# Layer 0 of a graph network on one core: the sums of a tile in two products over 33 rows of 17 terms, instead of three products over two arrays

## The reference, cut to what matters

```python
h = jnp.maximum(_layernorm(x, axis=-1), 0.0)
x = x + _L0_gnn_ref(h, edge_weight, edge_attr_3, edge_index, w1, b1, w2, b2)
h = jnp.maximum(_layernorm(x, axis=-1), 0.0)
x = x + _L1_gnn_ref(h, edge_index, W1, b1, W2, b2, W3, b3)   # three convolutions
# inside _L0_gnn_ref
R = jax.nn.relu(abs_distances[:, None] @ w1 + b1) @ w2 + b2
...
acc = acc + _NORM[i] * jnp.einsum('euv,ef,evi,ofi->euo', Rb[..., k], Yf, Fb, C)
...
out = out.at[dst].add(msg)
```

## Time and profile before

| what | value |
|---|---|
| runs | 8066.38 us median, 8041.97 to 8079.02 |
| span of the profiled execution | 8083.0 us, first to last instruction |
| PE busy, PE weight loads | 5256.2 us (65%), 3511.6 us (43%) |
| DVE, ACT, POOL busy | 3618.0 us, 2730.5 us, 3513.2 us |
| line 1926, the sums of layer 0, PE matmuls | 1134.5 us busy, 9408 records |
| line 1370, the reduction of the slots on DVE | 196 instructions |

### The profile page before, as it was taken

The page is one execution under the profiler, slowest core; times in us unless marked ns, Lnnn a source line. Parts: engine busy times, 40 slices in busy tenths (PEclk is TensorE's granted clock), DMA queues, the critical chain, the costliest instruction groups (busy, mean ns, idle before and its releaser), DMA issues.

```text
span 8083.0 us, 169450 instructions
## 1 busy us (share of the span) xinstructions
PE 5256.2 (65%) x62463; PEld 3511.6 (43%) x62464; DVE 3618.0 (45%) x8469; ACT 2730.5 (34%) x6550; POOL 3513.2 (43%) x3660
## 2 busy tenths in 40 slices
PE   4777677776767775554544557777777778455555
PEld 2444344443434443333333345555555556333333
DVE  6666566665656656444444442222222223333334
ACT  3333333333333333444444432222222223222222
POOL 5545445444444542444444434333333332444442
PEclk8877788787877776555555567887777788565566
DMA  2111111111111113222222221111111112222223
GB/s 66 26 26 27 24 26 27 26 26 24 27 24 26 26 25 37 59 55 55 55 55 55 55 80 55 57 56 53 56 55 53 55 55 83 68 79 81 78 82 87
DMA packets 494908, 400.37 MB, mean 50 GB/s; under 512 B 269575, under 2 KB 454828, under 8 KB 493537
## 3 DMA queue, kind: packets, MB, share of 16 engines
q10 hardware_dynamic: 146996, 207.67, 7.6%
q0 software_dynamic: 115712, 109.02, 7.1%
q1 hardware_dynamic: 231536, 74.48, 4.2%
HBM read 375.52 MB, written 15.29 MB: 48 GB/s over the span
## 4 chain that ended last, share of the span: by engine, by line
PE 38%; another core or an unknown queue 22%; DVE 18%; issue 17%; ACT 2%; DVEq 1%; DMA 1%; ACTq 0%; SPq 0%
PE radial L2051 14%; PE sums L1926 5%; DVE scratch L1344 4%; DVE scratch L1336 4%; PE sums L2137 4%; PE psX L2066 3%; PE psT L2066 3%; PE radial L1911 2%; PE psX L2069 2%; DVE scratch L1354 2%; PE psT L2069 1%; DVE shared L1310 1%; PE radial L2033 1%; PE radial L1908 1%
## 5 line engine op out<-in xcount | busy, mean ns | idle before, releaser
L768 POOL DMA_INDIRECT rows<-table,idx x3616 | 3486.8, 964 | 4415.6 <-PE sums L2137 2099.7
L2051 PE MATMUL radial<-arena,shared 128*32 128x96 bf16 (+1 forms) x31200 | 1469.7, 283 | 1072.6 <-issue 907.8
L2051 PEld LDWEIGHTS radial<-arena,shared 128*32 128x32 bf16 (+1 forms) x31200 | 848.1, 120 | 1551.6 <-issue 1311.4
L1926 PE MATMUL sums<-scratch,onehot 128*64 128x264 f32 (+1 forms) x9408 | 1134.5, 393 | 378.2 <-DVE scratch L1361 207.2
L1926 PEld LDWEIGHTS sums<-scratch,onehot 128*64 128x64 f32 x9408 | 818.2, 161 | 924.6 <-issue 480.7
L834 ACT ACTIVATE dist<-iota,rel 128x64 f32<-128x64 f32 (+1 forms) x2368 | 619.5, 342 | 1190.4 <-PE sums L1926 790.0
L1597 DVE TENSOR_SCALAR shared<-scratch,line 128x640 bf16<-128x640 bf16 (+1 forms) x906 | 408.3, 451 | 1367.9 <-remote 1102.7
L991 ACT CAST scratch<-radial 128x480 bf16<-128x480 f32 x860 | 470.8, 556 | 1593.4 <-remote 985.1
L1911 PE MATMUL radial<-shared 64*128 64x384 f32 x3136 | 880.9, 583 | 81.4 <-issue 77.8
L1336 DVE TENSOR_TENSOR scratch<-radial,shared 128x512 f32<-128x512 f32 x784 | 536.4, 684 | 740.4 <-remote 704.1
L1344 DVE TENSOR_TENSOR scratch<-radial,shared 128x768 f32<-128x768 f32 x784 | 741.6, 946 | 0.0
(11 more groups left out here) (236 smaller groups left out, 5445.4 us busy)
## 6 DMA issues: line engine op xcount, KB each, us to landing
scratch<-places_d ACTq DMA_DIRECT2D x242, 800.0 KB
rows<-table,idx POOLq DMA_INDIRECT x3616
shared<-in_edge_weight SPq DMA_DIRECT2D x390, 128.0 KB
idx<-in_src SPq DMA_DIRECT2D x451, 4.0 KB
table<-arena SPq DMA_DIRECT2D x24, 256.0 KB, 2.7
table<-arena SPq DMA_DIRECT2D x2, 1176.0 KB, 10.6
accT<-in_edge_attr SPq DMA_DIRECT2D x2, 1152.0 KB
table<-arena SPq DMA_DIRECT2D x24, 96.0 KB, 2.0
```

Source lines behind the costliest of these rows:

```text
L768: (pool.indirect_dma_start(rows_3[:, r, j, :] if n in (1, 3) else rows[:, r, j, 0:WIDTH[n]], None, tables[n], bass.IndirectOffsetOnAxis(ap ...
L1926: last = nc.tensor.matmul(there, onehot[:, u % 2, 4 * h + t, 0:SW], taken_from, start=(h + q + part == 0), stop=(h == 1 and q == 1 and par ...
L2051: last = nc.tensor.matmul(d, from_src[n][:, h, i, t, :], table_of(n, s), start=True, stop=True, tile_position=(0, 32 * i))
```

## The change

The two arrays become one: 8 scalar rows and 33 output rows of 17 terms each, `terms[..., row, term]`. Rows 0 to 7 are the scalars, rows 8 to 40 the outputs; term 16 of an output is what lay in the tail (a zero, the 1 of the count, or the direction term). A tile takes 17 x 41 = 697 values instead of 689. PE sums a tile in two products: first terms 8 to 16 into all 9 slots of each output (297 columns), then terms 0 to 7 into the first 8 of the 9 slots (264 columns). The rest follows from that: line 1370 reduces 33 x 9 slots, the DVE views have rows of 16 at a distance of 17, and line 1361 writes its 24 values of a tile 17 apart instead of next to each other. The far windows (a branch that is taken when a group's destinations don't fit in two windows of 64 nodes) use the same two products. No wait, no semaphore and no order between engines is changed.

```diff
-SEG0 = 16 * MUL
-TAIL0 = SEG0 + 16 * OUTS
-MSGW = TAIL0 + OUTS
-SUMW = 8 * OUTS
+TERMS = 17
+FIRST = MUL
+VECTOR = FIRST + MUL + 1
+MSGW = TERMS * (FIRST + OUTS)
+SLOTS_0 = 9
+SUMW = SLOTS_0 * OUTS
...
+        terms = scratch[:, 0:2 * 4 * MSGW].rearrange("p (h t m s) -> p h t m s", h=2, t=4, s=TERMS)
...
                     prod = v.tensor_tensor(
-                        msg[:, h, t:t + 2, 0:2 * SEG0].rearrange("p t (m s) -> p t m s", s=16),
+                        terms[:, h, t:t + 2, 0:2 * MUL, 0:16],
...
                     last = v.tensor_tensor(
-                        msg[:, h, t:t + 2, SEG0 + 16 * (MUL + 1):TAIL0].rearrange("p t (n s) -> p t n s", s=16),
+                        terms[:, h, t:t + 2, VECTOR:FIRST + OUTS, 0:16],
...
-                v.tensor_reduce(coef[:, h, :, :], msg[:, h, :, 0:SEG0].rearrange("p t (u s) -> p t u s", s=16),
+                v.tensor_reduce(coef[:, h, :, :], terms[:, h, :, 0:MUL, 0:16],
...
-                term = msg[:, h, :, TAIL0 + MUL + 1:MSGW].rearrange("p t (i u) -> p t i u", i=3)
+                term = terms[:, h, :, VECTOR:FIRST + OUTS, TERMS - 1].rearrange("p t (i u) -> p t i u", i=3)
...
-                v.tensor_reduce(nodes[:, :], sums[:, u % 2, 0:SUMW].rearrange("p (o s) -> p o s", s=8),
+                v.tensor_reduce(nodes[:, :], sums[:, u % 2, 0:SUMW].rearrange("p (o s) -> p o s", s=SLOTS_0),
...
-                slots = there.rearrange("p (o s) -> p o s", s=8)
-                terms = msg[:, h, t, SEG0:TAIL0].rearrange("p (o s) -> p o s", s=16)
-                if part == 2:
-                    return slots[:, :, 0], msg[:, h, t, TAIL0:MSGW]
-                return slots, terms[:, :, 8 * part:8 * part + 8]
+                slots = there.rearrange("p (o s) -> p o s", s=SLOTS_0)
+                summands = terms[:, h, t, FIRST:FIRST + OUTS, :]
+                return slots[:, :, 0:8 + part], summands[:, :, 8 * part:8 + 9 * part]
...
-                    for part in range(3):
+                    for part in (1, 0):
                         for w in range(2):
                             t = 2 * q + w
                             there, taken_from = window_part(sums[w * SW:(w + 1) * SW, u % 2, 0:SUMW], h, t, part)
                             last = nc.tensor.matmul(there, onehot[:, u % 2, 4 * h + t, 0:SW], taken_from,
-                                                    start=(h + q + part == 0), stop=(h == 1 and q == 1 and part == 2),
+                                                    start=(h + q == 0 and part == 1), stop=(h == 1 and q == 1 and part == 0),
                                                     tile_position=(0, w * SW))
```

More of the change, by code:

```diff
@@ L1242, in _ @@
             dve.wait_ge(table_out[0], 48)
-            link(v.memset(msg[:, :, :, SEG0 + 16 * MUL:SEG0 + 16 * MUL + 16], 0.0))
-            link(v.memset(msg[:, :, :, TAIL0:TAIL0 + MUL], 0.0))
-            link(v.memset(msg[:, :, :, TAIL0 + MUL:TAIL0 + MUL + 1], 1.0))
+            link(v.memset(terms[:, :, :, FIRST + MUL, 0:TERMS - 1], 0.0))
+            link(v.memset(terms[:, :, :, FIRST:FIRST + MUL, TERMS - 1], 0.0))
+            link(v.memset(terms[:, :, :, FIRST + MUL, TERMS - 1:TERMS], 1.0))
             dve.wait_ge(repeated, 2)
@@ L1288, in far_windows @@
                         if n == 0:
-                            v.tensor_reduce(nodesX[:, :], psX[:, 0:SUMW].rearrange("p (o s) -> p o s", s=8),
+                            v.tensor_reduce(nodesX[:, :], psX[:, 0:SUMW].rearrange("p (o s) -> p o s", s=SLOTS_0),
                                             X, ALU.add).then_inc(far_nodes, 1)
@@ L1881, in far_windows @@
                             if n == 0:
-                                for part in range(3):
+                                for part in (1, 0):
                                     there, taken_from = window_part(psX[:, 0:SUMW], j // 4, j % 4, part)
                                     last = nc.tensor.matmul(there, onehotX[:, j, :], taken_from,
-                                                            start=(j + part == 0), stop=(j == TPG - 1 and part == 2))
+                                                            start=(j == 0 and part == 1), stop=(j == TPG - 1 and part == 0))
                             elif far_rows[j] is not None:
```

## The result

The changed kernel takes 8219.61 us, the median of five runs (8170.37 to 8251.88), and the kernel before 8064.02 us in five runs beside them: a ratio of 1.019, 95% interval 1.0156 to 1.0224. It is slower, by 1.6 to 2.2%. The forecast was 8056 us with a range of 7985 to 8115. The profiled execution is the fastest of the five, so its trace shows the lighter part of the loss: a span of 8168.5 us against 8083.0.

The account below looks back on a forecast made before the run. Layer 0's loop was taken as bound by 10.04 us of gathers plus 5.45 us of waiting a group; PE's sums -13 and line 1370 +3 gave -10 us, 8056 us for the median, range 7985 to 8115.

Parts of the forecast that it names:

- The hold: Layer 0's loop: PE's updates reach other engines late during a run of gathers; 5.45 us a group from last gather to next.
- The changed work lies beside the loop, mostly under the hold.: Core of the forecast: no product for the sums stands in layer 0's loop; main case 8026 to 8106 us, chance 0.51.
- the -13 us: PE's sums on the chain: 7 us behind long stalls plus 6 us from half the other passages; bounds 0 and -74.
- more long stalls: Rival, layer 0's gathers: earlier PE makes runs of 16 more frequent; 12 more are +52 us, 8108 us; chance 0.14.
- PE's sums, -0.19 us a half: PE's products in the loop: four instead of six in a row lose a third of the fixed 0.56 us.
- The count of records: Sign of a right forecast: line 1926, PE's sums, with 6272 records.
- Line 1370, +34 ns: DVE's reduction over 297 instead of 264 elements: 6.7 us in all, half counted, +3 us.
- DVE's strides, 0: Lines 1336, 1344, 1354 and 1361 with new distances of 17: taken as 0, at most 116 us if all count.
- my bound for "wrong": Sign of a wrong forecast on DVE's strides: line 1361 above 300 ns.
- Writes with gaps: Rival, PE's second product skipping slots: +0.46 us a half, +44 us on the chain; chance 0.08, shared with DVE strides in full.

Follow-up runs that it names:

- ten and ten: Changed kernel with two products of 10 slots per tile, three terms added twice: ratio 1.0213; with GpSimd's wait ahead of the sixth gather 0.9339.
- the short third: Kernel before with three products per tile of 8, 5 and 1 slots, three of 17 terms left out of the sums: ratio 0.9991.
- padding: Changed kernel plus two unread 33-column products per pair of tiles, 24 records a half: ratio 1.0079; with GpSimd's wait ahead of the sixth gather 0.9761.
- the pause: GpSimd waits ahead of a group's sixth gather for the first radial product of four groups before: changed kernel 0.9327, kernel before 0.985.
- the tail left out: Kernel before without the third product of a tile (direction term and count of edges): ratio 1.0272.
- nine and nine: Changed kernel with both products of 9 slots, term 8 added twice: ratio 1.0223.
- three products over the new rows: Changed kernel keeping rows of 17 terms, but with three PE products per tile and 8 slots: 7976.84 us, ratio 0.9993.
- ScalarE's wait: ScalarE's last copy of gathered rows also waits for the first half's sums of two groups before: changed kernel 0.9533, kernel before 0.9732.

## Why the prediction was wrong, point by point

**What bounds the kernel.** The hold was read rightly but for one thing: an update can get out before POOL stops, as the one behind the DVE product at 1522.56 in the earlier trace rows did, which the working passes over. And it is stronger than I made it: a pause that lifts it once a group takes 6.8% off the kernel before (0.9323), with the change in it.

**The failed step.** "The changed work lies beside the loop, mostly under the hold." It treats the hold as fixed in time, ending with the gathers, so that less work of PE under it could only bring 0 to 74 us. But what PE executes after the gathers begin decides which of its updates still get through. With 24 records a half, the radial pairs behind the sums come at 27 and 33 records and are held, as in the earlier trace rows, the last to the run's end; that kept DVE and ACT back and with them POOL, in a rhythm mostly of 8 gathers. With 16, the first of them comes at 15 to 21 records and passes, the last passes too or gets out in the middle of the run, the next buffer is free early, and 16 gathers follow without a rest. So the -13 us had the wrong sign and the wrong size: layer 0 lost 81 us in the profiled execution, the median 156.

**The rival "more long stalls"** named this mechanism, its place and its sign, and had a chance of 0.14. Three things in it were off. Its cause was "PE that is 0.19 us earlier"; ten and ten and the short third refute that, and padding against ten and ten with the pause settles it. Its size: it took 12 more waits, and there were 45 more (82 for 37). And its price, 4.3 us each, was taken against two mean groups, in which the long runs are counted too. Each of 44 more runs of 16 takes 33.2 us for two runs of 8 at 14.99, +3.2 us and 141 in all; the 32 runs of 8 that are left win 1.49 us each, -48. That gives +93 us for the 81 that layer 0 lost in the profiled execution. The median lost 156; no profile of such an execution exists, so the rest of it is not shown, though the tail left out, nine and nine and ten and ten, at ratios of 1.021 to 1.027, have 78 to 83 runs of 16.

**PE's sums, -0.19 us a half**: 2.36 to 2.23 us at 2.4 GHz and 4.16 to 4.01 at 1.2 GHz, so -0.13 and -0.15. The count of records was right (6272).

**Line 1370, +34 ns**: 429 to 458, +29.

**DVE's strides, 0**: right for the rows of 16 at a distance of 17 (683 and 946 ns, from 684 and 946). The direction term went from 244 to 309 ns, +65 ns, just over my bound for "wrong". That is 0.68 ns an element, the low end of what the Trainium skill's "Vector Engine (DVE) Microarchitecture Reference", section 5.2, gives for a destination that hops at each element (0.66 to 1.45 ns above a contiguous one, an estimate from its table); the trace agrees with that end. In the whole it didn't count, as three products over the new rows show.

**Writes with gaps**: 465 ns with gaps against 482 without, and over the halves at 2.4 GHz alone 402 against 407. The rival charged the 162 ns by which the small record exceeds its share of columns to its scattered writes; the padding's product has 33 columns next to each other and takes 242 ns, the scattered one over the new rows 240, so that cost is not one of gaps. The rule of the Trainium skill's "PSUM — Partial Sum Buffer", specifications, that a non-contiguous access slows matmuls significantly, does not show in this case: a skipped slot after every 8 costs nothing here, and the measurement decides.

## What to carry to other kernels

Where several engines run round in a loop through semaphores, an engine with slack still sets the phase, and a saving there can turn an even pattern into a bunched one. Read the lengths of the runs of the slowest shared work, here how often POOL issues 8 gathers and how often 16, before and after, and forecast from them. If one change costs in such a loop, tie the source to what would bunch: one wait for PE per group took this kernel from 1.019 to 0.9327, and the change itself, a loss without it, is then worth 5.3% (0.9327 against 0.985).

## What the runs showed of the hardware

While GpSimd issues indirect gathers back to back, PE keeps executing, but its semaphore updates stop reaching the other engines in time once some 22 to 27 of its matmul records, with as many weight loads, have passed since the first gather. They arrive up to 8.1 us late in a run of 8 gathers and 17.6 us late in one of 16. The updates of DVE and ACT are not held: of those over 5 us into a run of gathers whose moment the changed kernel's trace has, 240 of DVE and 81 of ACT, none was over 0.6 us late, and of PE's 390 of 392 were.

When a held update gets out differs. In the kernel before, of 645 held ones 188 came over 0.5 us before the last gather's end, as the one behind 1522.56 in the earlier trace rows did, 44 within 0.5 us of it, and 386 came 1.0 to 3.2 us behind it; in the pause alone the last kind is at 1.0 to 2.1 us. A short break doesn't end the hold: in the kernel before, eight updates that came 0 to 3 records into a run, after a break of 1.52 to 1.60 us, were held for 9.1 to 10.8 us.

What is counted (matmuls, loads, or instructions of PE) and which part of the chip holds the updates back stays open: no run here separates these. Nor is the count a sharp bound: in the changed kernel 39 of 76 updates at 20 to 23 records were held, where the pause alone has 15%, and four at 15 records, 3.6 to 4.8 us into a run.

The fastest version is the changed kernel with the pause: 7445.73 us with it ahead of the fourth gather and ScalarE's wait, and 7447.87 us ahead of the sixth without ScalarE's wait. The two can't be told apart.
